# A fused attention and expert kernel: batch 0's expert gates spread over the partitions by DMA, batch 1's exponential of the routing logits computed by POOL

## The reference, cut to what matters

```python
x = x + attn(cond(x, cond_1024, weight), w_qkv, w_out)                       # "x1" below
x = x + ffn(cond2(x, cond_1024, ...), W1, b1, W2, b2, Wa, Wb)

# cond2: per token, 2 shared experts and 8 routed ones of which 2 count
s = sigmoid(concat([x, t], -1) @ W_router.T)                                 # t: the condition, per batch
idx = top_k(s + router_bias, 2);  s_sel = s[idx]
gates = s_sel / (sum(s_sel) + 1e-9)                                          # 0 for the other 6 experts
shared = sum_e (silu(x @ s_w1[e].T) * (x @ s_w3[e].T)) @ s_w2[e].T / 2
routed = sum_e (gelu(x @ r_w1[e].T) @ r_w2[e].T) * gates[:, e]
out = (shared + routed) / 4
```

## Time and profile before

| what | us |
| --- | --- |
| median of 3 runs (197.03 to 198.95) | 197.34 |
| the profiled execution, whole | 197.56 |
| its span, first to last instruction | 195.8 |
| PE busy in the span (1006 matmuls) | 180.1 |
| DVE busy (459 instructions) | 143.7 |
| ACT busy (228) | 137.9 |
| POOL busy (97) | 83.6 |

### The profile page before, as it was taken

How to read it: one execution, slowest core, us unless ns; L and a number is a source line. 1 busy time by engine, 2 the same in 40 slices (tenths; PEclk the granted TensorE clock), 3 DMA queues, 4 the chain that set the end, 5 groups by cost and what they waited for, 6 DMA issues and landing times.

```text
span 195.8 us, 3320 instructions
## 1 busy us (share of the span) xinstructions
PE 180.1 (92%) x1006; PEld 124.1 (63%) x1006; DVE 143.7 (73%) x459; ACT 137.9 (70%) x228; POOL 83.6 (43%) x97
## 2 busy tenths in 40 slices
PE   7897698999999999898999999999799989999992
PEld 3654364666656666664467685786467857788881
DVE  5589699889898989896167974679969657556642
ACT  4479255486867768698843874576778899899880
POOL 4517359343324546464620620202467950497000
PEclk9999999999999999999999999999999999999999
DMA  4927657767585769431110899000000000001001
GB/s 143 363 85 229 203 189 233 205 176 223 161 264 157 223 184 253 141 96 54 54 50 5 274 310 311 5 2 0 0 2 3 0 0 0 0 2 57 0 0 54
DMA packets 13985, 23.06 MB, mean 118 GB/s; under 512 B 2632, under 2 KB 3784, under 8 KB 13912
## 3 DMA queue, kind: packets, MB, share of 16 engines
q1 hardware_dynamic: 13392, 22.46, 37.1%
q10 hardware_dynamic: 576, 0.39, 0.6%
HBM read 17.42 MB, written 6.09 MB: 120 GB/s over the span
## 4 chain that ended last, share of the span: by engine, by line
PE 61%; DVE 15%; ACT 11%; issue 6%; DMA 3%; SPq 2%; POOL 1%; DVEq 0%; ACTq 0%; POOLq 0%
PE psum L1414 9%; PE psum L1291 8%; PE psum L1416 8%; PE psum L1415 8%; PE psum L1342 7%; PE psum L1322 5%; DVE psum L680 3%; DMA t_q_pad<-scratch 2%; PE psum L1235 2%; PE psum L1249 2%; PE psum L1181 2%; DVE t_raw L826 2%; PE psum L1325 2%; ACT t_q_pad L1044 1%; DVE t_raw L830 1%
## 5 line engine op out<-in xcount | busy, mean ns | idle before, releaser
L680 DVE CUSTOM_DVE_ANT_0 psum<-psum,t_causal 128x128 f32<-128x128 f32 (+3 forms) x128 | 59.3, 525 | 8.0 <-PE psum L1291 7.3
L992 ACT ACTIVATE t_probs<-psum 128x768 f32<-128x768 f32 (+1 forms) x48 | 41.0, 880 | 4.9 <-PE psum L1322 3.3
L1291 PE MATMUL psum<-t_stacked,t_q_pad 128*128 128x256 f32 (+2 forms) x128 | 37.3, 361 | 3.9 <-issue 1.7
L576 POOL TENSOR_SCALAR_AFFINE_SELECT t_probs<-t_probs 128x512 f32<-128x512 f32 x32 | 20.0, 636 | 31.6 <-ACT t_probs L992 28.4
L1291 PEld LDWEIGHTS psum<-t_stacked,t_q_pad 128*128 128x128 f32 x128 | 21.4, 188 | 18.8 <-DVE t_row_max L680 10.8
L844 DVE SCALAR_TENSOR_TENSOR t_q_pad<-psum,t_zw_all,t_q_pad 128x512 fp32r<-128x512 f32 x24 | 17.9, 749 | 11.7 <-ACT t_q_pad L1042 11.6
L1028 ACT ACTIVATE t_raw<-psum 128x512 f32<-128x512 f32 x24 | 14.3, 595 | 10.4 <-PE psum L1460 7.7
L1342 PE MATMUL psum<-t_probs,t_v_all 128*32 128x512 f32 (+3 forms) x256 | 20.5, 439 | 0.0
L612 POOL TENSOR_TENSOR t_q_pad<-t_raw,t_q_pad 128x512 fp32r<-128x512 f32 x8 | 10.3, 1288 | 20.1 <-ACT t_q_pad L1044 20.1
L1322 PE MATMUL psum<-t_q_mov,t_k_pad 128*128 128x512 f32 (+1 forms) x64 | 18.4, 373 | 0.2
L680 DVE DVE_READ_ACCUMULATOR2_ANT t_row_max<- 128x1 f32 x128 | 18.4, 144 | 0.0
(11 more groups left out here) (228 smaller groups left out, 389.8 us busy)
## 6 DMA issues: line engine op xcount, KB each, us to landing
t_stacked<-scratch SPq DMA_DIRECT2D x14, 256.0 KB, 3.6
t_probs<-in_L_ffn_Wa SPq DMA_DIRECT2D x2, 1024.0 KB, 8.3
t_q_pad<-scratch SPq DMA_DIRECT2D x28, 64.0 KB, 3.2
t_k_pad<-scratch SPq DMA_DIRECT2D x28, 64.0 KB, 2.2
scratch<-t_o_sb SPq DMA_DIRECT2D x7, 256.0 KB, 2.0
t_raw<-in_experts SPq DMA_DIRECT2D x7, 256.0 KB, 3.4
scratch<-t_dn_hi SPq DMA_DIRECT2D x4, 256.0 KB
scratch<-in_rest SPq DMA_DIRECT2D x2, 448.0 KB
```

What stands on the lines that cost most here:

```text
L576: last = G.affine_select(out=tri, in_=tri, compare_op=ALU.is_ge, fill=0.0, base=0, pattern=[[0, HG], [1, P]], channel_multiplier=-1)
L680: last = V.tensor_tensor_reduce(scores, scores, causal[:, S - width:S], 1.0, 3 * BIG, ALU.add, ALU.max, row_max[s][:, qb, j:j + 1])
L992: A.activation(probs[s][:, c, 2 * h2:2 * h2 + 2, 0:w], ST[:, slot_of("exp", n, u):slot_of("exp", n, u) + 2, 0:w], ACT.Exp, scale=float(1.0 ...
L1291: last = T.matmul(ring("max", n, u)[:, i * 2 * P:i * 2 * P + width], q_pad[s][:, j, qb * P:(qb + 1) * P], stacked[:, 2 * n + 1, 0:width], ...
```

## The change

Batch 0's gates take another way. `gates(0, 3)` stops after the unsplit gate. PE turns the 128x8 tiles, ACT copies the 8x512 result into `o_sb[0]` and now does so before `hidden_hi(0)` (it was after `activate(1)`). SP writes these 8 rows to DRAM and reads each back with a source repeated 128 times, into 8 tiles of 128x512 in the buffer `stacked`; each load has a semaphore of its own. `finish_hidden` of batch 0's routed units waits for its load and multiplies two tiles in SBUF. The selection matmul and the wait for the pair's second bank go for these 8 units. Batch 1's gates stay as they were.

`spread_inverse` is split: SP stores batch 1's inverse sums behind the store of the gates, waits for the gates' store, then loads `packed_sum`, then issues the 8 gate loads, then the zones' weights.

Batch 1's exponential leaves ACT. DVE writes the negated logits to SBUF at i = 11, POOL raises e to them with one `pow` over 128x32 after x1's low part, and `gates(1, 0)` waits for that. Of POOL's two memsets of `gates_t` one goes.

```diff
-    "copy gates": [1, 15],
+    "copy gates": [0, 15],
-    "exp 1": [11],
+    "logits 1": [11],
...
-        gates_t = [q_pad[b][:, RING, :] for b in range(B)]
+        gates_t = q_pad[1][:, RING, :]
+        gate_rows_b0 = o_sb[0][0:EXPERTS, :]
+        gate_of = [f32_of(stacked[:, 2 * NG + e, :]) for e in range(EXPERTS)]
+        gate_dram = scratch[GROUPS][B * H:B * H + EXPERTS, :]
+        neg_logits, e_neg1 = (sb(x, [P, KB, EXPERTS]) for x in ("neg_logits", "e_neg1"))
+        e_neg[1] = e_neg1[:]
...  SP
             gather(1)
+            def load_gate(e):
+                sp.dma_start(gate_of[e], gate_dram[e:e + 1, :].broadcast_to([P, S])).then_inc(ld_gate[e], 16)
+            sp.wait_ge(gateT_copied, 1)
+            sp.dma_start(gate_dram, gate_rows_b0).then_inc(gates_out, 16)
+            store_inverse(1)
+            sp.wait_ge(gates_out, 16)
             spread_inverse(1)
+            for e in range(EXPERTS):
+                load_gate(e)
...  POOL, at unit 12 of its list, behind x1_lo of batch 1
+                    pool.wait_ge(euler_ready, 1)
+                    pool.wait_ge(negated, 1)
+                    G.tensor_tensor(e_neg[1], euler[:], neg_logits[:], ALU.pow).then_inc(expneg, 1)
...  DVE
+            def negate_logits():
+                dve.wait_ge(logits, B)
+                V.tensor_scalar(neg_logits[:], MISC[:, 0:KB * EXPERTS].rearrange("p (t e) -> p t e", t=KB), -1.0, None,
+                                ALU.mult).then_inc(negated, 1)
...
-                    step(V.tensor_tensor(gate[b], part_s[b], part_c[:, b], ALU.add))
+                    last = V.tensor_tensor(gate[b], part_s[b], part_c[:, b], ALU.add)
+                    if b == 0:
+                        last.then_inc(gate_ready, 1)
+                        return
+                    step(last)
...
-                    V.tensor_tensor(hidden_of(i), act_out[r], pair[:, 1, :], ALU.mult).then_inc(h_ready, 1)
+                    if b == 0:
+                        dve.wait_ge(ld_gate[w], 16)
+                    V.tensor_tensor(hidden_of(i), act_out[r], pair[:, 1, :] if b else gate_of[w],
+                                    ALU.mult).then_inc(h_ready, 1)
...
+                for _ in due("logits 1", i):
+                    negate_logits()
                 for part in due("gates 1", i):
                     gates(1, part)
...  ACT
+                    act.wait_ge(stored[0], 16 * (GROUPS // 2))
+                    A.copy(gate_rows_b0, psum[0:EXPERTS, 7 - b, :]).then_inc(gateT_copied, 1)
...
             activate(0)
             copy_pv(GROUPS - 1)
+            gates_t_copy(0)
             hidden_hi(0)
...
-                for _ in due("exp 1", i):
-                    exp_of_minus_logits(1)
...  PE, in up(i)
-                    if kind == "routed":
+                    if kind == "routed" and b:
                         if w == 0:
                             pe.wait_ge(gateT_copied, b + 1)
                             pe.wait_ge(sele_ready, 1)
                         second_bank_free()
-                        last = T.matmul(pair_of(i)[:, 1, :], sel_e[:, w, :], gates_t[b], start=True, stop=True)
+                        last = T.matmul(pair_of(i)[:, 1, :], sel_e[:, w, :], gates_t, start=True, stop=True)
```

More of the change, by code:

```diff
@@ L298, in program @@
          x12_ready, z_hid, z_tanh, z_logit, z_step, z_diff, z_exp, z_w, z_bc, z_all, a_hi, b_hi, a_lo, b_lo, y_ready,
-         stored_y, euler_ready) = (sems[n] for n in names)
+         stored_y, euler_ready, negated, gates_out) = (sems[n] for n in names)
         q_padded = [sem(f"q_padded{s}") for s in range(2)]
@@ L304, in program @@
         stored = [sem(f"stored{s}") for s in range(2)]
+        ld_gate = [sem(f"ld_gate{e}") for e in range(EXPERTS)]
         xc_ready = [sem(f"xc_ready{k}") for k in range(3)]
@@ L457, in gather, with store_inverse @@
                 sp.dma_start(packed_out[0:rows, :], heads[:, 0:HD, :]).then_inc(packed, 16)
-            def spread_inverse(b):
+            def store_inverse(b):
                 rows = EARLY if b else P
@@ L465, in spread_inverse @@
                 sp.dma_start(inverse.rearrange("h (c t) -> (h c) t", c=HD), sums[0:rows, b, :]).then_inc(inv_stored, 16)
+            def spread_inverse(b):
+                rows = EARLY if b else P
+                heads = rows // HD
+                inverse = scratch[GROUPS][b * H:b * H + heads, :]
                 sp.wait_ge(inv_stored, 16 * (b + 1))
@@ L500, in _ @@
                 if n == NG:
+                    store_inverse(0)
                     spread_inverse(0)
@@ L597, in _ @@
                 if n == GROUPS - 2:
-                    for b in range(B):
-                        pool.wait_ge(mx_full, GROUPS * MXU)
-                        G.memset(f32_of(gates_t[b]), 0.0).then_inc(gates_zero, 1)
+                    pool.wait_ge(mx_full, GROUPS * MXU)
+                    G.memset(f32_of(gates_t), 0.0).then_inc(gates_zero, 1)
             for i in LO_POOL:
@@ L1047, in gates_t_copy @@
                 act.wait_ge(gateT_full, b + 1)
-                act.wait_ge(gates_zero, B)
-                A.copy(gates_t[b][0:2 * EXPERTS, :], psum[0:2 * EXPERTS, 7 - b, :]).then_inc(gateT_copied, 1)
+                if b:
+                    act.wait_ge(gates_zero, 1)
+                    A.copy(gates_t[0:2 * EXPERTS, :], psum[0:2 * EXPERTS, 7 - b, :]).then_inc(gateT_copied, 1)
+                else:
+                    act.wait_ge(stored[0], 16 * (GROUPS // 2))
+                    A.copy(gate_rows_b0, psum[0:EXPERTS, 7 - b, :]).then_inc(gateT_copied, 1)
             def finish_experts(b):
@@ L1072, in router_tanh, with exp_of_minus_logits @@
                              bias=small[0:RH, W_B1:W_B1 + 1]).then_inc(z_tanh, 1)
[L1074 to L1077, removed]
+            def exp_of_minus_logits():
+                act.wait_ge(logits, 1)
+                bank = ring("route", 0)[:, 0:KB * EXPERTS]
+                A.activation(e_neg[0], bank.rearrange("p (t e) -> p t e", t=KB), ACT.Exp,
                              scale=-1.0).then_inc(expneg, 1)
@@ L1133, in _ @@
                 if n == GROUPS - 1:
-                    exp_of_minus_logits(0)
+                    exp_of_minus_logits()
                 exp(n, 5)
@@ L1494, in transpose_gates @@
                 for t in range(KB):
-                    last = T.transpose(psum[:, 7 - b, :][0:2 * EXPERTS, t * P:(t + 1) * P], gate_hl[:, b, t, :],
-                                       f32_of(ident_r[:]))
+                    tokens = slice(t * P, (t + 1) * P)
+                    if b:
+                        last = T.transpose(psum[0:2 * EXPERTS, 6, tokens], gate_hl[:, b, t, :], f32_of(ident_r[:]))
+                    else:
+                        last = T.transpose(psum[0:EXPERTS, 7, tokens], gate[0][:, t, :], f32_of(ident_r[:]))
                 last.then_inc(gateT_full, 1)
```

4 lines of the change are left out of this document (1 added, 3 removed).

## The result

The changed kernel takes 201.92 us (median of 6 runs, 201.49 to 202.49) against 197.53 us for the kernel before on the same chip (6 runs). The ratio is 1.0214 with a 95% interval of 1.0175 to 1.0252: slower by 4.4 us between the medians, 4.2 by the ratio. The forecast had 200.8, with a range of 197.2 to 205.2. The difference that the two traces have to explain is 3.9 us.

A forecast was written before the change was run, and what follows sets the result against it. PE bounds batch 0's routed experts, DVE's batch 1 gates bound 129 to 141 us. Gates 3.8 us later less 0.4 gives +3.4 on 197.56, 201.0; less 0.2 to the median, 200.8, range 197.2 to 205.2.

The forecast's parts named there:

- the sum: Whole kernel: +3.8 us at batch 1's gates, -0.4 behind them, so +3.4 on the profiled 197.56.
- The pow: POOL, ahead of batch 1's gates: 0.41 + 32 x 0.148 = 5.15 us; gates begin 3.8 us later.
- (a): Between negation and gates: pow cheap, up to 1.8 us; 196.4 to 197.3, not slower; chance 0.22.
- (b): Same place: pow between 1.8 and 3.5 us, as where columns overlap; up to +1.8, 199.1; chance 0.09.
- The path to it: Batch 0's gates to the pow: `project_out(1)` 0.44 us earlier at 117.9, router 0.90 earlier at 124.65, pow at 129.05.
- Products beside POOL: DVE products of units 5 and 10, two SBUF inputs: stand behind POOL's subtraction, near 1.4 us, others 0.69.
- The gate loads: SP's queue: 0.68 us per further load, gate 0 at 112.0 with 0.9 us spare that grows; costed at nothing.
- Rival (c): Gate loads late: 1.5 us each called harmless; at 2.0 us the last is 4 us late, 204; chance 0.09.
- rival (d): PE stands some 5.4 us, clock falls to 1.2 GHz, matmuls double: up to +4, 204.8; chance 0.15.
- What came back: Behind batch 1's gates: ACT's table load back to gelu, 1.28 us, goes; 0.4 us counted.

The follow-up runs named there:

- the DMA gates alone: The changed kernel with batch 1's exponential back on ACT, without pow or negation for batch 1: 196.29 us, ratio 0.9956.
- The probe: The kernel before with four more pows of 128x4, 128x8, 128x16 and 16x16 on POOL, results unread: 198.56 us in a single run.
- gelu in PSUM: Batch 0's routed gelu written to the pair's second PSUM bank: on the changed kernel 201.49 us; on DMA gates with batch 1's sigmoid by tanh 195.06 us.
- the clock held: The changed kernel with unit 14's first-tile matmuls issued eight times more on PE, same result: 202.26 us, ratio 1.02.
- the pow alone: The kernel before with batch 1's exponential as negation plus pow on POOL, batch 0's gates unchanged: 203.23 us, ratio 1.031.
- the tanh: Batch 1's sigmoid as 0.5 + 0.5 tanh(x/2) on ACT: on the DMA gates 195.29 us, on the kernel before 196.64 us.
- the gates moved: The changed kernel with batch 1's four gate parts two units later in DVE's order (13, 14, 14, 15): 204.34 us, ratio 1.0312.

## Why the prediction was right, point by point

- **The time.** 200.8 forecast, 201.92 measured; in the profiled executions +3.4 forecast, +3.9 found. Of the 1.1 us between the medians, 0.5 is that; 0.2 is the correction from 197.56 to 197.34, where the median of the later runs is 197.53; and 0.4 is that the profiled execution of the changed kernel is the fastest of its six. The mechanism was the forecast one, DVE's wait for the pow ahead of batch 1's gates. With the DMA gates alone the span is 1.0 us shorter, and the pow on top of them adds 4.9. The pow without them adds 5.9, so the two parts don't simply add up; the 1 us between is mostly the longer low clock.
- **The 0.5 us, term by term.** Pow 0.29 longer, its start 0.07 later, 0.24 for the clock ahead of the turn, which the sum had at nothing, and 0.45 back behind the turn instead of 0.4.
- **The pow.** The line through two small rows gave 5.15 us, it took 5.44: the fixed 0.41 was right, the column costs 0.157 instead of 0.148. So a slope from two rows one column apart, of which one has a single partition, was 6% off over 32 columns; that it came so near is also luck, as two rows can't show that the line is straight. The probe shows it from 4 to 32, with no overlap of columns and no effect of partitions, which ends rivals (a) and (b).
- **The path to it.** `project_out(1)` was forecast for 117.9 and came at 117.93, the router for 124.65 and came at 124.67, POOL's pow for 129.05 and came at 129.12. The prediction says first that only the matmuls of units 8, 9 and 11 count, and later gives units 4 to 6 their 0.69 us and takes it back (0.21 for POOL's low parts, 0.48 for the product that stands); the two agree only through that. At `project_out(1)` nothing of the 0.69 is left, as forecast: PE's waits there and at the router grew to 0.68 and 0.61 us, from 0.37 and 0.38. That trace runs 0.11 us late already at 104.35, where 104.24 stood before, so the path gained slightly more than I had it.
- **Products beside POOL.** Forecast 1.4 us for units 5 and 10; measured 1.23 and 1.38. With one input in PSUM they take 0.70, so the cause is shown. The rule of the Trainium skill that the prediction cites ("SBUF — State Buffer", section "SBUF: two separate sides") and these rows agree. The other direction, POOL held by DVE, shows once: with the DMA gates alone POOL's subtraction at 113.36 took 1.48 us instead of 1.28, and DVE's product of unit 4 had begun at 113.00, ahead of it.
- **The gate loads.** Wrong in one step, with no effect on the time of the changed kernel. I priced each further load at 0.68 us by 384 GB/s and wrote that the spare grows. Two stretches of the changed kernel, in which mainly these loads move (`packed_sum` ahead of them, and toward the end a zone's weights), have less:

```profile
110.00:112.00 2.00, 1.34 (x8) 0.92 (x7) 1.93 (x5) 1.58 (x3) 1.77 (x2) 1.00 0.83 257
112.00:114.00 2.00, 2.00 (x14) 1.77 (x13) 1.69 (x3) 1.90 (x4) 0.87 (x2) 1.00 0.88 252
```

The last column is GB/s: at that rate 256 KB take about 1.0 us, and SP issues a load every 0.43 us, so they queue, 3.4 us from issue to landing at best and 7.1 at worst. Gate 0 had landed by 113.00, when its product began. Its spare of 0.9 us was mostly gone in another version: with the DMA gates alone no load took less than 4.5 us, so gate 0, issued at 108.34, landed at 112.84 at the earliest, and its product began at 113.00, 0.17 us behind the moment at which DVE was free for it. For gate 1 the spare is gone: with the gelu in PSUM it landed at 114.1 on one version, 0.85 us after DVE was ready for it, and by 113.68 on the other, whose product began there released by ACT. In the changed kernel it landed by 114.17, when its product began 0.03 us behind ACT's activation. Behind that the spare does grow: the last load was issued at 111.9, landed by 119.0 (at most 7.1 later), and its product begins at 127.60. Rival (c) didn't happen, by less than I had. Its own sum is also off in one place: with 1.5 us a load the last gate would come 0.6 us late by the formula given, which isn't harmless.
- **The clock.** It fell to 0.50, as rival (d) has it, and that rival's price was wrong. I had up to 4 us; PE alone lost 1.7, and of it 0.24 reached the turn of the gates (PE 4.35 us later there, its releaser on DVE 4.11). With the clock held at 1.00 that delay is gone, and the rest of the program is 0.12 us shorter. DVE is what the stretch waits for. The sum had nothing for the clock; it is 0.24 here, and 1.08 with the pow alone (1.33 less 0.25).
- **What came back.** I counted 0.4 us for the second table load, and that was right. From the turn of batch 1's gates to the end of the last computing instruction it is 54.08 us in the changed kernel and with the pow alone, 54.14 and 54.15 in the versions with the clock held and with the gelu in PSUM; with the load it is 54.53 in the kernel before and 54.56 with the DMA gates alone. So 0.45 us comes back behind the turn. DVE's start of the gates is 4.14 us later, the clock adds 0.24 up to the turn, the load gives back 0.45: 3.9, the whole difference.

## What to carry to other kernels

Before an operation is moved to an engine that is mostly idle, price it there by its columns, and look at what its result holds up: POOL was busy for 43% of the span, and still its 5.44 us for 32 columns of pow cost 5 us, where ACT's table switch had cost about 1. Here a function from a table that was already loaded was worth more than the idle engine: the tanh took 0.21 us and no load. And an instruction order written by hand has to be moved as a whole chain, consumer by consumer; one entry moved alone made this kernel slower.

## What the runs showed that was not expected

- A DVE operation with one SBUF input can stand behind POOL too: with the gates moved, L777 (`tensor_scalar`, 128x32, SBUF to SBUF) took 1.25 us beside POOL's subtraction and 0.18 us otherwise; the reciprocal behind it, also from SBUF to SBUF, took its usual 0.35. In "SBUF — State Buffer", section "Who interferes with whom", the Trainium skill counts `tensor_scalar` among the operations that can take the port pair that DVE shares with GpSimd, when their operands meet its conditions; this row agrees.
- DVE's 128x32 addition L780 with two SBUF inputs took 0.84 us beside POOL, 0.20 alone.
- Loads of one repeated DRAM row, 256 KB each at the destination, moved some 255 GB/s, where the earlier trace rows have 384 with other loads. The comparison is loose: the kernel before has 288 to 384 GB/s in stretches of 2 us between 110 and 116.
- PE stood 5.63 us, and the clock was 0.50 for the 3.6 us behind it; in the trace of the kernel before, whose longest wait is 1.7 us, it is 1.00 in every stretch of 10 us.
